# Where the small recurrence's h is made, and a DMA that exchanges the halves of its block Q

## The reference, cut to what matters

```
def lstm_last(x, Wx, Wh, b):
    def step(carry, xt):
        h, c = carry
        g = xt @ Wx + h @ Wh + b
        i, f, gg, o = jnp.split(g, 4, axis=-1)
        c = sigmoid(f) * c + sigmoid(i) * tanh(gg)
        h = sigmoid(o) * tanh(c)
...
m_from = lstm_last(base_emb[from_seq], seq_Wx, seq_Wh, seq_b)
m_to   = lstm_last(base_emb[to_seq],   seq_Wx, seq_Wh, seq_b)
nwf    = vmap(enc)(...11 features..., nums, freqs)      # x = two looked-up rows of 4, 32 steps, H = 8
feats  = concatenate([small embeddings, m_from, m_to, more small embeddings, nwf])
return relu(feats @ reduce_W + reduce_b)
```

## Time and profile before

| | us |
|---|---|
| median of 3 runs | 1870.71 |
| the profiled execution | 1870.87 |
| its span, first to last instruction | 1869.1 |
| PE busy | 1699.5 (91%) |
| ACT busy | 1488.3 (80%) |
| DVE busy | 1423.0 (76%) |
| POOL busy | 929.2 (50%) |
| chain that ended last, PE's share | 73% |
| chain that ended last, ACT's share | 12% |

### The profile page before, as it was taken

One profiled execution on the slowest core, in us unless ns is written; L12 is line 12 of the kernel. 1 busy time (PEld: TensorE's weight loads), 2 busy tenths in 40 slices (PEclk: granted clock), 3 DMA queues, 4 the chain that ended last, 5 costly groups with the idle time before them and its releaser, 6 DMA issues.

```text
span 1869.1 us, 59759 instructions
## 1 busy us (share of the span) xinstructions
PE 1699.5 (91%) x25092; PEld 780.9 (42%) x25092; DVE 1423.0 (76%) x1279; ACT 1488.3 (80%) x2579; POOL 929.2 (50%) x476
## 2 busy tenths in 40 slices
PE   2157989999999999999999999999999999999995
PEld 2112434444444444444444444444444444444444
DVE  7056668888888788888888888887888888888871
ACT  3235768888888888888888888888888888898883
POOL 7435874445444444545444544545444544545442
PEclk9578999999999999999999999999999999999997
DMA  6696778888888888888888898888888888888831
GB/s 171 103 311 207 233 228 287 283 267 282 276 289 267 279 281 287 275 272 280 284 276 276 277 285 279 283 275 278 284 274 270 288 279 283 276 276 280 283 133 46
DMA packets 166154, 484.24 MB, mean 259 GB/s; under 512 B 53213, under 2 KB 104959, under 8 KB 120831
## 3 DMA queue, kind: packets, MB, share of 16 engines
q1 hardware_dynamic: 163327, 480.27, 78.1%
q0 software_dynamic: 2560, 0.15, 1.2%
HBM read 474.04 MB, written 6.09 MB: 257 GB/s over the span
## 4 chain that ended last, share of the span: by engine, by line
PE 73%; ACT 12%; issue 5%; POOL 1%; DMA 1%; DVE 1%; SPq 0%; DVEq 0%; POOLq 0%
PE ab L648 31%; PE e_ps L571 19%; PE f_ps L648 11%; ACT gate L688 9%; PE ab L598 8%; PE ab L535 3%; ACT tanh_c L688 1%; ACT f_ps L697 1%; ACT gate L697 1%; DMA last_h<-nwf_h 0%; PE e_ps L924 0%; POOL ig L718 0%; POOL small_rows L281 0%; DVE kept L583 0%; DMA low<-last_h 0%
## 5 line engine op out<-in xcount | busy, mean ns | idle before, releaser
L718 POOL TENSOR_TENSOR ig<-gate 128x1024 f32<-128x1024 f32 x192 | 410.8, 2140 | 842.6 <-ACT seq_x L542 568.3
L561 DVE TENSOR_SCALAR hot<-low,cst 128x4096 bf16<-128x4096 bf16 x352 | 451.4, 1283 | 170.4 <-PE e_ps L571 166.3
L571 PE MATMUL e_ps<-hot,tab 128*32 128x512 bf16 x8448 | 529.7, 385 | 26.4 <-DVE kept L583 26.2
L583 DVE SCALAR_TENSOR_TENSOR kept<-high,cst,e_ps 128x1024 f32<-128x1024 uint8 x352 | 449.1, 1276 | 28.8 <-PE e_ps L571 20.0
L648 PE MATMUL ab<-seq_h,seq_wh 64*64 64x512 f32 x3072 | 409.3, 592 | 0.0
L571 PEld LDWEIGHTS e_ps<-hot,tab 128*32 128x32 bf16 x8448 | 204.8, 97 | 409.3 <-issue 251.1
L745 POOL TENSOR_TENSOR seq_h<-gate,tanh_c 128x1024 f32<-128x1024 f32 x128 | 303.7, 2373 | 19.6 <-ACT tanh_c L688 19.6
L695 ACT ACTIVATE gate<-ab 128x1024 f32<-128x1024 f32 x256 | 262.9, 1027 | 17.6 <-PE ab L648 11.7
L688 ACT ACTIVATE tanh_c<-seq_c 64x512 f32<-64x512 f32 (+1 forms) x384 | 241.5, 629 | 12.8 <-DVE seq_c L731 9.7
L688 ACT ACTIVATE gate<-ab 64x512 f32<-64x512 f32 (+1 forms) x384 | 228.4, 595 | 11.5
L697 ACT ACTIVATE gate<-ab,nwf_bias 128x256 f32<-128x256 f32 (+1 forms) x384 | 147.4, 456 | 104.3 <-PE ab L648 100.2
(11 more groups left out here) (77 smaller groups left out, 1674.7 us busy)
## 6 DMA issues: line engine op xcount, KB each, us to landing
low<-low_digits SPq DMA_DIRECT2D x352, 1024.0 KB, 7.3
tok<-seq_tokens SPq DMA_DIRECT2D x128, 384.0 KB, 4.7
high<-high_digits SPq DMA_DIRECT2D x1408, 32.0 KB, 3.4
nwf_in<-in_r_nwf_numbers SPq DMA_DIRECT2D x1, 2816.0 KB, 13.8
nwf_in<-in_r_nwf_freqs SPq DMA_DIRECT2D x1, 2816.0 KB, 21.0
low_digits<-turned SPq DMA_DIRECT2D x8, 352.0 KB, 5.5
high_digits<-turned SPq DMA_DIRECT2D x8, 160.0 KB
low<-last_h SPq DMA_DIRECT2D x11, 64.0 KB
```

Source lines behind the costliest of these rows:

```text
L561: nc.vector.tensor_scalar(hot[:, p % HOT_RING, :, :].rearrange("p u c -> p (u c)"), low[:, p % LOW_RING, :, :].rearrange("p u c -> p (u c) ...
L571: last = nc.tensor.matmul(e_ps[32 * g:32 * g + 32, i, :], tab[:, part, 2 * m + ty, :], hot[:, p % HOT_RING, i, g * CH:(g + 1) * CH], start ...
L583: nc.vector.scalar_tensor_tensor(out=kept[:, p % KEPT_RING, :, :].rearrange("p u c -> p (u c)"), in0=high[:, p % HIGH_RING, :, :].rearrang ...
L718: nc.gpsimd.tensor_tensor(ig[:, n % 2, cols], gates[0][:, n % 2, cols], gates[1][:, n % 2, cols], ALU.mult).then_inc(ig_ready, 1)
```

## The change

For nwf, h is now made where its gates lie. ACT writes gate o and tanh(c) in place: gate o in four instructions of 128 x 256 for part 0 (two for part 1: 128 x 256 and 128 x 128), tanh(c) in one (128 x 1024, or 128 x 384). h of block P is as before; h of block Q comes out with its halves swapped. SP then exchanges the halves by two DMAs into a new buffer `nwf_hq` (`move_q`), which PE reads for block Q. It does so for steps 0 to 30 of each part, so 62 times, two cells behind. PE's first matmul of an nwf cell also waits for that exchange (`q_moved`), and so does POOL before it overwrites h. At the end `regroup_h` writes block Q in two halves, three DMAs in place of two. POOL clears the new buffers at the start. The seq cells are as before.

```
@@ -427,6 +427,8 @@
 
         seq_h = sb("seq_h", [P, 2, 2, CH], F32, work)
         nwf_h = [sb(f"nwf_h{k}", [P, p[1] + q[1]], F32, work) for k, (p, q) in enumerate(PARTS)]
+
+        nwf_hq = [sb(f"nwf_hq{k}", [P, q[1]], F32, work) for k, (p, q) in enumerate(PARTS)]
         seq_c = sb("seq_c", [P, 2, 2 * CH], F32, work)
         nwf_c = [sb(f"nwf_c{k}", [P, p[1] + q[1]], F32, work) for k, (p, q) in enumerate(PARTS)]
         nwf_x = sb("nwf_x", [P, 2, COLS], F32, work)
@@ -468,6 +470,7 @@
         c_ready = sem("c_ready")
         tanh_ready = sem("tanh_ready")
         h_ready = sem("h_ready")
+        q_moved = [sem(f"q_moved{k}") for k in range(2)]
         state_set = sem("state_set")
         nwf_w_ready = sem("nwf_w_ready")
         h_in_dram = [sem(f"h_in_dram{c}") for c in range(2)]
@@ -628,6 +631,8 @@
                     ab_is_done(pe, ("x", step, 3 if k == 0 else 5))
                 if step:
                     at_least(pe, h_ready, NUMBER[kind, step - 1, k] + 1)
+                    if kind == "nwf":
+                        pe.wait_ge(q_moved[k], 32 * step)
             if g == FORGET:
 
                 at_least(pe, c_ready, n)
@@ -650,6 +655,8 @@
                 return last
 
             def h_rhs(rows, block, a, b):
+                if kind == "nwf" and block:
+                    return nwf_hq[k][rows, a:b]
                 return h[rows, wp * block + a:wp * block + b]
 
             if kind == "seq":
@@ -703,7 +710,10 @@
 
             at_least(act, h_ready if g == 3 else ig_ready, n - 1)
             to, of = gates[g][:, n % 2, in_sbuf(n)], flat(ab[USE[what] % 2])[:, in_psum(n)]
-            last = at_h(to, of, pieces(n, g), GATES[g][1]) if g == 3 else in_place(to, of, n, g)
+            if g == 3 and CELLS[n][0] == "seq":
+                last = at_h(to, of, pieces(n, g), GATES[g][1])
+            else:
+                last = in_place(to, of, n, g)
             last.then_inc(ab_done, 1)
 
         def activate_f(act, n):
@@ -735,13 +745,20 @@
             wp, wq = widths(n)
             at_least(act, c_ready, n + 1)
             at_least(act, h_ready, n - 1)
-            at_h(tanh_c[:, n % 2, in_sbuf(n)], c_of(n), [(0, 0, wp, None), (1, wp, wq, None)],
-                 ACT.Tanh).then_inc(tanh_ready, 1)
+            if CELLS[n][0] == "seq":
+                last = at_h(tanh_c[:, n % 2, in_sbuf(n)], c_of(n), [(0, 0, wp, None), (1, wp, wq, None)], ACT.Tanh)
+            else:
+                last = nc.scalar.activation(tanh_c[:, n % 2, in_sbuf(n)], c_of(n), ACT.Tanh)
+            last.then_inc(tanh_ready, 1)
 
         def new_h(pool, n):
             cols = in_sbuf(n)
             at_least(pool, tanh_ready, n + 1)
             ab_is_done(pool, ("gate", n, 3))
+            kind, step, k = CELLS[n]
+            if kind == "nwf" and step:
+
+                pool.wait_ge(q_moved[k], 32 * step)
             nc.gpsimd.tensor_tensor(h_of(n), gates[3][:, n % 2, cols], tanh_c[:, n % 2, cols],
                                     ALU.mult).then_inc(h_ready, 1)
 
@@ -754,6 +771,15 @@
                 cst[src, None, C_DIAG:C_DIAG + 64].rearrange("p o (s u) -> p o s u", u=8)
                 .to_broadcast([64, NSETS * 4, 8, 8]), ALU.mult).then_inc(nwf_w_ready, 1)
 
+        def move_q(sp, n):
+
+            _, step, k = CELLS[n]
+            wp, wq = widths(n)
+            sp.wait_ge(h_ready, n + 1)
+            for half in range(2):
+                sp.dma_start(nwf_hq[k][64 * half:64 * half + 64, :], nwf_h[k][64 - 64 * half:128 - 64 * half, wp:wp + wq]
+                             ).then_inc(q_moved[k], 16)
+
         def load_later(sp, p):
             if p < ALL_PAIRS:
                 load_pair(sp, p)
@@ -762,10 +788,13 @@
             kind, step, k = "nwf", NWF_T - 1, part
             queue.wait_ge(h_ready, NUMBER[kind, step, k] + 1)
             (pat, wp, _), (qat, wq, _) = PARTS[k]
-            for at, w, a in ((pat, wp, 0), (qat, wq, wp)):
-                queue.dma_start(h_dram[:, :, at:at + w].rearrange("s u c -> (s u) c"),
-                                nwf_h[k][:, a:a + w]).then_inc(h_in_dram[k], 16)
-            queue.wait_ge(h_in_dram[k], 32)
+            queue.dma_start(h_dram[:, :, pat:pat + wp].rearrange("s u c -> (s u) c"), nwf_h[k][:, 0:wp]
+                            ).then_inc(h_in_dram[k], 16)
+            for half in range(2):
+
+                queue.dma_start(h_dram[8 * half:8 * half + 8, :, qat:qat + wq].rearrange("s u c -> (s u) c"),
+                                nwf_h[k][64 - 64 * half:128 - 64 * half, wp:wp + wq]).then_inc(h_in_dram[k], 16)
+            queue.wait_ge(h_in_dram[k], 48)
             for j in range(min(pat, qat) // LANES, (min(pat, qat) + wp + wq) // LANES):
                 queue.dma_start(rest[NWF_H * j:NWF_H * j + NWF_H, :, :],
                                 h_dram[:, :, j * LANES:(j + 1) * LANES].rearrange("s u b -> u s b")
@@ -788,6 +817,8 @@
                     s = later_seq(n)
                     if s is not None and s + 2 < 2 * SEQ_T:
                         load_tokens(sp, s + 2)
+                    if n >= 2 and CELLS[n - 2][0] == "nwf" and CELLS[n - 2][1] + 1 < NWF_T:
+                        move_q(sp, n - 2)
                 ab_is_done(sp, ("small",))
                 for s in range(4):
                     sp.dma_start(rest[FEATURES * NWF_H:REST, s::4, :],
@@ -837,6 +868,7 @@
                 nc.gpsimd.memset(seq_c[:, :, :], 0.0)
                 for k in range(2):
                     nc.gpsimd.memset(nwf_h[k][:, :], 0.0)
+                    nc.gpsimd.memset(nwf_hq[k][:, :], 0.0)
                     last = nc.gpsimd.memset(nwf_c[k][:, :], 0.0)
                 last.then_inc(state_set, 1)
                 for n in range(NCELLS):
```

10 lines of the change are left out of this document (6 added, 4 removed).

## The result

| | before | after |
|---|---|---|
| median, us | 1871.07 (4 runs) | 1840.26 (4 runs, 1837.37 to 1842.30) |
| ratio of the runs | | 0.9832, 95% interval 0.9815 to 0.9849 |
| the profiled execution, its span | 1870.87, 1869.1 | 1839.72, 1837.9 |

The kernel became 1.7% faster: 31 us, where the prediction said 22. Every ratio in this document leaves out runs over 1.5% above the fastest of their kernel, which happened only to two of the six runs with doubled exchanges.

A forecast was written before the change was run, and what follows sets the result against it. PE was taken as the bound, busy 1176.51 of 1200 us, with its waits for gate o to be saved. The profiled 1870.87 - 25.1 + 3.3 gave 1849.1 (1848.9 against the median), stated as 1849 us; range 1844 to 1860.

The forecast's parts named there:

- Gate o in place: PE's waits at line 598 behind nwf cells, 0.50 us in part 0, 0.36 in part 1, go whole: -25.1 us.
- With 0.14 us to spare: Part 1: gate o would end early enough for PE to start at 931.71, with PE ready at 931.85.
- Tanh in place: tanh(c) of nwf in one piece, 1.07 and 0.52 us; only POOL waits for it in the rounds, worth 0.
- The exchange in the rounds: Exchanges delay each next `low` load by 0.85 us, covered by slack before DVE and PE need the data: 0.
- the third semaphore: PE's added wait at the first matmul of an nwf cell: taken as 0, bounds 0 and 8.7 us.
- The end: Last cells: PE stands still 4.5 us for the last exchange; with tanh, slower matmuls, copies and `regroup_h`, +3.3 us.
- the clock: Last cell: PE's first matmuls behind the 4.5 us stall run at the 1.2 GHz level, +1.6 us (bounds 0 and 2.2).
- The four copies of small rows: SP's list at the end: they stand behind the last exchange, about 1835.5 to 1840.5; taken as 0.2 us.
- end costs nothing: Rival, chance 0.13: clock stays at 1.00 and the last exchange lands quicker than a DRAM write; 1846.5, or 1845 us.
- The ramp: Before the rounds: the 0.50 us gained at 213.40 is waited away again at 225.69, by way of `kept`.
- ACT's time was never what PE waited for: Rival, chance 0.06: the wait is only labelled gate o and all turns into waiting for `kept` or DVE; 1874 us.

The follow-up runs named there:

- doubled exchanges: The changed kernel with each exchange of steps 0 to 29 issued a second time, into a buffer PE doesn't read; ratio 0.9873 (first four of six runs).
- part 1 alone: The kernel before with gate o written in place for nwf part 1 only, nothing exchanged; 1856.39 us, 0.9920.
- without exchanges: The changed kernel without its 62 exchanges and the waits for them, PE reading block Q from `nwf_h`; 1833.41 us, 0.9792.
- gate o alone: The kernel before with gate o of both nwf parts written in place, tanh left in three pieces, nothing exchanged; 1832.28 us, 0.9790.
- the repeated run: The changed kernel, unedited, measured once more on one chip beside POOL's swap of the halves; 1844.92 us, 0.9828, its profiled execution 1849.8 us.

## Why the prediction was wrong, point by point

**Gate o in place: the step that failed.** "Part 0: 0.50 us ... part 1 for 0.36 us", 25.1 us together. The mechanism was right, with the durations (1.57 and 0.73 us, to the hundredth). The term was mis-sized: the waits measured 0.70 and 0.49. With about 30 of the one and 28 of the other, that is 34.7 us instead of 25.1. Put into the prediction's own sum: 1870.87 - 34.7 + 3.3 = 1839.5, beside 1839.72 measured. The agreement is partly luck, since an earlier ramp (-0.9) and short stalls (+1.9) are in the measurement. The rows that would have told it, 1.31 us from start to start where nothing waited against 1.97, were in the trace of before.

**"With 0.14 us to spare" in part 1.** By the same error it was not to spare: PE was ready 0.13 us earlier than the bracket said. After, PE starts 0.15 us behind the end of gate o (914.61 + 0.73 = 915.34, start 915.49), the lag of a wait, and 0.05 later than in an unwaited place. So a rest of the wait is there, and no bracket shows it. The kernel with part 1 alone agrees.

**Tanh in place, 0.** Right (52.58 against 52.61 in the round). It took 1.06 us (1806.73 above) and 0.53 for the estimates of 1.07 and 0.52:

```profile
L751 ACT ACTIVATE tanh_c<-nwf_c 128x384 f32<-128x384 f32 x32 | 17.0, 531 | 4.3 <-DVE nwf_c L741 4.3
```

**The exchange in the rounds, 0.** Right for the profiled execution: the third semaphore costs nothing, PE never waits for an exchange in the rounds, and they are as long as without exchanges. Not right for every execution: in the one of 1849.8 us `low` came late and some 8 us were lost. The argument was too light. Bytes are not what such a transfer costs the DMA engines; the share of 0.92 and the doubled exchange show how little room was left. In the rounds 128 KB landed 4.5 us behind their issue in the middle, and 32 KB in 4.3, nearly the same for a fourth of the bytes. The last exchange of part 1, at the end and with no 1 MB load beside it, landed in 1.90 us (the row below, from the chain that ended last). The Trainium skill (DMA: Bandwidth & Descriptors, Anatomy of one DMA), in a section on transfers issued by GpSimd, gives a fit of about 2.0 us fixed plus little for so few bytes. SP issues the exchange here; the trace agrees at the end, with 1.90, and not in the rounds, with 4.5.

```profile
1800.76 1.90 DMA nwf_hq<-nwf_h
```

**The end, +3.3.** Measured +3.6 to the predicted +3.8 in the same stretch. Inside it: the stall 4.25 (4.5 predicted); gate i begins 3.19 us behind PE's start at 0.58 of the clock (2.24 + 1.6 = 3.84 predicted), so the clock cost 0.95 and not 1.6; the end of tanh of part 0 comes 2.05 us later behind the small rows than before (3.0 predicted, with the clock), the rest another 1.5 later (0.8 predicted). Most of that is the third DMA of `regroup_h`: from the first issue of a part to the start of its last DMA it is 0.96 us (1810.26 to 1811.22) where it was 0.40 (1843.00 to 1843.40), about 0.5 more in each part. The landings are little longer: 2.35 for 2.32 us, and 5.75 for 5.56 (1849.02 in the chain of before). The four copies of small rows cost nothing, since they were issued by 1806.33. The rival "end costs nothing" fell. One reading was off: the 2.32 us of the earlier trace rows start at 1843.40, the second issue, and not at the first at 1843.00; the exchange took 1.90 from its second issue. The first of SP's rows in the timeline, and the chain of the kernel after (start, us, what; part 0, then part 1):

```profile
1810.26 0.35 SPq L791 DMA_DIRECT2D last_h<-nwf_h  x1
...
1811.22 2.35 DMA last_h<-nwf_h
...
1817.36 5.75 DMA last_h<-nwf_h
```

**The ramp, 0.** The prediction that the 0.50 gained at 213.40 is waited away again was right: the wait for `kept` at 225.69 grew from 1.36 to 1.88 us. The stretch to the first mark came 1.5 us earlier; 0.66 of it is gate o's wait (1.97 against 1.31 us from start to start), and the lookup ahead of it comes 0.85 earlier. That lies within what the other kernels show there, so no cause is given.

```profile
224.66 1.48 PE L574 MATMUL e_ps<-hot,tab 128*32 128x512 bf16 x24 [1.88 <-DVE kept L586]
```

**Short stalls.** After 300 us the changed kernel has six stalls beyond its round, 2.9 us together; the kernel before has two, 1.0 us; without exchanges they are 2.65 us, with gate o alone 0.8. The profile puts those that show a bracket down to "issue". What they are stays open; stalls of this size come without exchanges too. The 9.1 us of the repeated run are another thing: most of them lie where DVE waits for `low`.

**The range** left this out because it bounded the unknown costs and took the known gain as exact. It rested on a label of the profile, and the rival that dealt with the label ("ACT's time was never what PE waited for") looked only at its being too large.

## What to carry to other kernels

Size a wait of TensorE from the start of the group before it to the start of the group behind it, and compare with the same pair of groups in a place where nothing waits; the idle time in brackets counts from a modelled end and gave 0.50 for 0.70 us. An exchange by DMA that PE doesn't wait for where two cells cover it is the whole path in the last step, where the old form does better in the trace. Before adding small transfers, look at the busy share of the DMA engines and not at the bytes.

## What the runs showed of the hardware

- The exchanges of a round, four DMAs of 64 partitions and 320 KB together, 2% of the bytes, raised the DMA engines' share by 0.05 (0.87 to 0.92). Doubled, the share was 0.97, and in another execution of the changed kernel it was 1.01 for 220 us: in both DVE waited for loads.
- POOL's product of 64 x 512 took 2.07 us in mean, that of 128 x 512 1.30, and that of 128 x 1024 2.37. Half the partitions, taken from the other half, cost 1.6 times as much as all of them. That of 64 x 128 took 0.46 us.
- The granted clock behind a stall of PE at the end: 1.00 behind 1.67 and 2.26 us, 0.58 behind 4.25 (in the ramp, 0.57 behind 2.41). Behind a stall of 2.45 us it was 0.72 in one kernel, and behind one of 2.46 us 1.00 in another, so the length of the stall alone doesn't tell it.
